# Column tiles for the query-key-value product, attended values a step later, style on ScalarE and merged exponent rounds

## What is computed

```python
def layer0(x, c, positions):                       # conditioned attention block
    sh1, sc1, g1, sh2, sc2, g2 = split(c @ ada_w.T + ada_b, 6)
    h = rmsnorm(x) * (1 + sc1) + sh1
    q, k, v = split(h @ qkv_w.T)                   # then q, k: rmsnorm by head, rotated by positions
    o = softmax(q @ k.T / sqrt(8)) @ v
    x = x + g1 * (o @ proj_w.T + proj_b)
    h2 = rmsnorm(x) * (1 + sc2) + sh2
    return x + g2 * (silu(h2 @ w1.T) * (h2 @ w3.T) @ w2.T)

def layer1(x, emb, gate):                          # linear attention
    q, k, v = layer_norm(x) @ (Wq, Wk, Wv) + (bq, bk, bv)
    y = softmax_d(q) @ (softmax_n(k).T @ v)
    h = layer_norm(y) * (1 + scale) + shift        # scale, shift = silu(emb) @ emb_W + emb_b
    return x + gate * (silu(h) @ out_W + out_b)
```

## Time and profile before

| what | before |
|---|---|
| median of three runs | 207.35 us |
| the profiled execution | 207.43 us, its span 205.4 us |
| TensorE (PE) busy | 180.9 us, 88% of the span |
| VectorE (DVE) busy | 166.1 us, 81% |
| GpSimd (POOL) busy | 141.3 us, 69% |
| ScalarE (ACT) busy | 129.4 us, 63% |
| granted TensorE clock | full in all 40 slices |
| chain that ended last, by engine | PE 40%, DVE 17%, issue 8%, POOL 5%, ACT 4% |

### The profile page before, as it was taken

How to read it: one execution, slowest core, us unless ns; L and a number is a source line. 1 busy time by engine, 2 the same in 40 slices (tenths; PEclk the granted TensorE clock), 3 DMA queues, 4 the chain that set the end, 5 groups by cost and what they waited for, 6 DMA issues and landing times.

```text
span 205.4 us, 6100 instructions
## 1 busy us (share of the span) xinstructions
PE 180.9 (88%) x2039; PEld 142.3 (69%) x2039; DVE 166.1 (81%) x498; ACT 129.4 (63%) x377; POOL 141.3 (69%) x333
## 2 busy tenths in 40 slices
PE   2598887997999999799999998899998899999963
PEld 2345565786687777677676777799997677888642
DVE  6699898896989999997776534668889799999882
ACT  1367798776867777576546763454442468999741
POOL 8889798998989797958810682434542847668651
PEclk9999999999999999999999999999999999999999
DMA  5955006800000000000000000000000000010111
GB/s 93 289 137 207 0 10 254 359 6 0 3 3 2 5 5 0 3 0 5 3 3 0 5 0 3 0 0 5 2 0 2 0 3 0 0 30 28 51 51 51
DMA packets 10428, 8.30 MB, mean 40 GB/s; under 512 B 3106, under 2 KB 9887, under 8 KB 9887
## 3 DMA queue, kind: packets, MB, share of 16 engines
q1 hardware_dynamic: 7006, 7.25, 10.3%
q10 hardware_dynamic: 3392, 0.68, 1.7%
HBM read 6.86 MB, written 1.07 MB: 39 GB/s over the span
## 4 chain that ended last, share of the span: by engine, by line
PE 40%; DVE 17%; issue 8%; POOL 5%; ACT 4%; POOLq 0%; ACTq 0%; DVEq 0%
PE bank L1895 5%; DVE qkpad L1604 5%; PE bank L875 5%; PE bank L1886 5%; PE bank L863 5%; PE bank L864 4%; PE bank L1975 4%; ACT probs L1302 2%; PE bank L908 2%; POOL rstd L515 2%; PE bank L1907 1%; PE bank L1920 1%; PE bank L992 1%; PE bank L1949 1%; PE bank L972 1%
## 5 line engine op out<-in xcount | busy, mean ns | idle before, releaser
L1604 DVE TENSOR_REDUCE qkpad<-bank 128x4 f32<-128x512 f32 x64 | 41.0, 684 | 10.1 <-PE bank L1886 9.2
L1302 ACT ACTIVATE probs<-bank 128x512 f32<-128x512 f32 x64 | 34.7, 594 | 22.6 <-PE bank L1895 22.5
L1895 PE MATMUL bank<-qTm,kBD 32*128 32x128 f32 x512 | 37.1, 283 | 0.1
L1886 PE MATMUL bank<-kBD,qTs 32*128 32x256 f32 x224 | 32.0, 399 | 4.4 <-DVE qkpad L1604 3.4
L1895 PEld LDWEIGHTS bank<-qTm,kBD 32*128 32x128 f32 x512 | 31.0, 186 | 0.9 <-issue 0.6
L1886 PEld LDWEIGHTS bank<-kBD,qTs 32*128 32x128 f32 x224 | 19.7, 184 | 10.3 <-DVE qkpad L1604 6.3
L575 ACT ACTIVATE th<-bank 128x256 f32<-128x256 f32 x24 | 9.2, 384 | 19.4 <-PE bank L864 16.0
L1975 PE MATMUL bank<-probs,vpad 128*32 128x128 f32 x512 | 18.6, 277 | 2.0 <-ACT probs L1302 2.0
L1975 PEld LDWEIGHTS bank<-probs,vpad 128*32 128x32 f32 x512 | 12.6, 109 | 8.4 <-ACT probs L1302 7.3
L1130 POOL TENSOR_TENSOR partner<-qk,rope 128x96 f32<-128x96 f32 x32 | 14.4, 471 | 2.0 <-ACT qk L1344 2.0
L1949 PE MATMUL bank<-qkvT,hT 128*128 128x384 f32 x32 | 15.3, 571 | 0.5 <-ACT hT L1319 0.5
(11 more groups left out here) (253 smaller groups left out, 521.4 us busy)
## 6 DMA issues: line engine op xcount, KB each, us to landing
gate<-in_cond_dram SPq DMA_DIRECT2D x1, 1024.0 KB, 4.7
x<-gate_rows SPq DMA_DIRECT2D x1, 1024.0 KB, 4.3
y<-gate_rows SPq DMA_DIRECT2D x1, 1024.0 KB, 6.4
res<-gate_rows SPq DMA_DIRECT2D x1, 1024.0 KB, 9.8
out_dram<-res SPq DMA_DIRECT2D x7, 128.0 KB, 1.8
xin<-in_x_dram ACTq DMA_DIRECT2D x2, 256.0 KB, 5.4
xin<-in_x_dram SPq DMA_DIRECT2D x1, 512.0 KB, 5.7
ada_n<-in_L_cond_ada_w_dram SPq DMA_DIRECT2D x1, 256.0 KB, 6.2
```

What stands on the lines that cost most here:

```text
L1302: q.activation(probs[2 * r + i][:, :, :, :].rearrange("p f a t -> p (f a t)"), bank[E_BANK[i]][:, :], ACT.Exp, scale=SCALE).then_inc(s_p, 1)
L1604: q.tensor_reduce(out_, score_bank(b, r, i)[:, :].rearrange("p (f a t) -> p f a t", f=2, a=2), X_AXIS, ALU.max, negate=True).then_inc(s_ma ...
L1886: last = q.matmul(bank[S_BANK[i]][:, f * 2 * T:(f + 1) * 2 * T], qTs[b % 2][rows, f, :], kBD[b % NKB][rows, f, :, :].rearrange("p a t -> p ...
L1895: last = q.matmul(bank[E_BANK[i]][:, (2 * f + k) * T:(2 * f + k + 1) * T], kBD[t % NKB][rows, f, k, :], qTm[t % 2][rows, f, :], start=True ...
```

## The change

The change has these parts:

- `queries_keys_values`: from sequence 6 on, the product is made in four tiles of 32 stationary columns each, with all 384 moving columns for each tile.
- `attended`, `projection`, `gated_projection`, `after_attention` and `spread_of` work on sequences one step older (t-2 and t-3), the attention loop has one step more (`LAST_A = B + 3`), and `oT` has two buffers. TensorE's `attended` stands behind round 0 and not ahead of the weighted values; ScalarE's stands between the two exponents of round 0.
- `queries_and_keys` and `input_turned` come directly behind that, ahead of `projection`, `token_major` and `queries_and_max`.
- The masked queries `qTs` of sequences from 3 on are made by ScalarE.
- In steps 14 and 15, where there are no scores left, one call `exponents` computes all inputs, with 4 row groups side by side; its second half goes to banks 0 and 1. The feed-forward chunks therefore use banks 4, 0, 1 and not 0, 1, 4, and chunks 1 and 2 wait for all exponents.
- `style`: one operation stays on VectorE, in step 0; the broadcast and the scaled weights are made on ScalarE at the end of step 10. `prepare_biases` moves to t = 11, 12 and 13.

```diff
-LAST_A, LAST_POOL = B + 2, B + 1
+LAST_A, LAST_POOL = B + 3, B + 1
...
-        GU_BANK, F_BANK, X_BANK = (0, 1, 4), (2, 3), 7
+        GU_BANK, F_BANK, X_BANK = (4, 0, 1), (2, 3), 7
...
+        def exp_bank(b, r, i):
+            return bank[(S_BANK if r == 1 and b + 2 >= B else E_BANK)[i]]
...
+                    if c > 0 and at(u, 0):
+                        e.wait_ge(s_p, NC * B)
...
+            def queries(b):
...
+                a.wait_ge(s_kb, b - MASKED_BY_ACT + 1)
+                q.activation(qTs[b % 2][:, :, :].rearrange("p f t -> p (f t)"), bank[T_BANK][:, 0:2 * T], ACT.Identity,
+                             scale=rowmask[:, 0:1]).then_inc(s_kq, 1)
...
             for t in range(LAST_A):
                 exp(t, 0, 1)
+                attended(t - 2)
                 exp(t, 0, 0)
...
+                modulated_input(t + 6)
                 queries_and_max(t + 1)
-                modulated_input(t + 6)
+                queries(t + 3)
                 exp(t, 1, 0)
                 exp(t, 1, 1)
-                if t < B:
-                    attended(t - 1)
...
-                spread_of(t - 2)
+                spread_of(t - 3)
                 if t == B - 6:
                     a.wait_ge(ld_rest, N_REST)
                     q.activation(outw[:, :], outw_n[:, :], ACT.Copy, scale=0.5).then_inc(pv_a, 1)
-            blocks_scalar(a, 2)
+                    q.activation(nbb[:, :], ident[:, :], ACT.Identity, bias=par[:, R_NB:R_NB + 1], scale=0.0).then_inc(pv_a, 1)
+                    q.activation(lin[:, :, :].rearrange("p c f -> p (c f)"), lin_n[:, :, :].rearrange("p c f -> p (c f)"), ACT.Identity,
+                                 scale=par[:, R_NG:R_NG + 1]).then_inc(pv_a, 1)
+            blocks_scalar(a, LAST_A - B)
...
                 rowmax(t + 2, 0, 1)
+                keys_apart(t + 3)
                 reciprocals(t - 1)
-                gated_projection(t - 2)
                 attended(t - 1)
-                keys_apart(t + 3)
-                queries(t + 3)
+                gated_projection(t - 3)
...
-                after_attention(t - 2)
+                after_attention(t - 3)
...
-                if t == B - 8:
                     style()
...
+            def exponents(t):
+                e.wait_ge(s_qTm, t + 1)
+                e.wait_ge(s_max, NC * B)
+                e.wait_ge(s_p, NC * t)
+                for f in range(2):
+                    for k in range(2):
+                        for r in range(2):
+                            for i in range(2):
...
+                    for c in range(4):
+                        last = q.matmul(front_bank(b)[32 * c:32 * c + 32, 128:512], hT[b % 2][:, 32 * c:32 * c + 32], qkvT[:, :],
+                                        start=True, stop=True)
...
             for t in range(LAST_A):
-                round_(t, 0)
-                projection(t - 2)
+                if t < B - 2:
+                    round_(t, 0)
+                elif t < B:
+                    exponents(t)
+                attended(t - 2)
+                queries_and_keys(t + 3)
+                input_turned(t + 6)
+                projection(t - 3)
                 token_major(t - 1)
...
-                queries_and_keys(t + 3)
-                input_turned(t + 6)
-                if B - 6 <= t < B - 3:
-                    prepare_biases(t - (B - 6))
+                if B - 5 <= t < B - 2:
+                    prepare_biases(t - (B - 5))
...
-                round_(t, 1)
+                if t < B - 2:
+                    round_(t, 1)
                 queries_keys_values(t + 6)
-                if t < B:
-                    attended(t - 1)
                 weighted_values(t, 0)
+                weighted_values(t, 1)
                 if t == B - 1:
                     b_rest(t - B, t % 2)
-                weighted_values(t, 1)
                 if t >= B:
                     b_input(t - B, t % 2)
                     b_rest(t - B, t % 2)
-                    attended(t - 1)
-            blocks_tensor(e, 2)
+            blocks_tensor(e, LAST_A - B)
```

More of the change, by code:

```diff
@@ L1361, in attended @@
                 a.wait_ge(s_oTp, b + 1)
-                wait(a, s_proj, b)
-                q.activation(oT[:, :], bank[P_BANK][:, 256:384], ACT.Copy).then_inc(s_oT, 1)
+                wait(a, s_proj, b - 1)
+                q.activation(oT[b % 2][:, :], bank[P_BANK][:, 256:384], ACT.Copy).then_inc(s_oT, 1)
             def summed(b):
@@ L1836, in prepare_biases @@
                 if part == 0:
[L1837 removed]
+                    e.wait_ge(pv_a, A_STYLE)
+                    e.wait_ge(pv_v, V_CSILU)
                     e.wait_ge(s_v, B)
@@ L1898, in round_ @@
                                     last.then_inc((s_e0, s_e1)[i], 1)
+            def exponents(t):
[6 more added lines that the diff above has]
+                            for i in range(2):
+                                row = 32 * (2 * r + i)
+                                rows = slice(row, row + 32)
+                                last = q.matmul(exp_bank(t, r, i)[:, (2 * f + k) * T:(2 * f + k + 1) * T], kBD[t % NKB][rows, f, k, :],
+                                                qTm[t % 2][rows, f, :], start=True, stop=True)
+                                if f == 1 and k == 1:
+                                    last.then_inc((s_e0, s_e1)[i], 1)
             def projection(b):
@@ L1904, in projection @@
                 e.wait_ge(s_oT, b + 1)
-                e.wait_ge(s_oT4, min(b + 2, B))
+                e.wait_ge(s_oT4, min(b + 3, B))
                 wait(e, s_x1g, b)
-                q.matmul(bank[O_BANK][:, 0:D], oT[:, :], projT[:, :], start=True, stop=True).then_inc(s_proj, 1)
+                q.matmul(bank[O_BANK][:, 0:D], oT[b % 2][:, :], projT[:, :], start=True, stop=True).then_inc(s_proj, 1)
             def token_major(b):
@@ L1948, in queries_keys_values @@
                 e.wait_ge(s_hT, b + 1)
-                q.matmul(front_bank(b)[:, 128:512], hT[b % 2][:, :], qkvT[:, :], start=True, stop=True).then_inc(s_qkv, 1)
+                if b < FRONT_B:
+                    q.matmul(front_bank(b)[:, 128:512], hT[b % 2][:, :], qkvT[:, :], start=True, stop=True).then_inc(s_qkv, 1)
+                else:
+                    for c in range(4):
+                        last = q.matmul(front_bank(b)[32 * c:32 * c + 32, 128:512], hT[b % 2][:, 32 * c:32 * c + 32], qkvT[:, :],
+                                        start=True, stop=True)
+                    last.then_inc(s_qkv, 1)
             def queries_and_max(b):
@@ L1966, in weighted_values @@
                     wait(e, s_on, b)
-                    wait(e, s_x1g, b - 1)
+                    wait(e, s_x1g, b - 2)
                     if b == 0:
@@ L1984, in attended @@
                 wait(e, s_qTm, min(b + 3, B))
+                wait(e, s_oT, b)
                 q.transpose(bank[P_BANK][:, 256:384], o[:, :, :].rearrange("p h d -> p (h d)"), ident[:, :]).then_inc(s_oTp, 1)
```

45 lines of the change are left out of this document (22 added, 23 removed).

## The result

The changed kernel takes 209.11 us (median of 12 runs, 208.92 to 209.94) against 207.37 us before: ratio 1.008, 95% interval 1.0062 to 1.0098. The forecast was 209.2. The profiled execution takes 209.30 us with a span of 207.57 (before 207.43 and 205.42).

A forecast was written before the change was run, and what follows sets the result against it. TensorE, busy 88%, was taken to wait for others, with ScalarE's exponents a 2.99 us floor under the half from round 1. Terms -1.06 + 1.38 + 0.64 - 0.43 + 1.29 = +1.82 on 207.43 gave 209.2 us, range 206.3 to 211.4.

The forecast's parts named there:

- the floor of 2.99: From round 1 to the next round 0, ScalarE's exponents allow no less than 2.99 us; 3.07 falls only to that.
- The rival that TensorE's saving counts: Front steps gain 0.3 us each, merged rounds 1.1 each, if exponents do not hold the values: 204.2 us; chance 0.12.
- that of strict order: Rival: column tiles run strictly one after another, the product takes 1.6 us, ten steps lose 7 us: 216; chance 0.04.
- First half longer by the evacuation: Round 0 to round 1: ScalarE's evacuation between the two exponents delays round 1, 2.66 us in place of 2.55, +0.11.
- Wait for GpSimd in step 3: Queries' and keys' transposes wait for GpSimd with more work queued behind them: +0.63 us, bounds 0 and 1.0.
- VectorE's relief: Masked queries moved to ScalarE shorten steps where VectorE makes seeds: -0.16, -0.09 and -0.26 us up to step 10.
- Style: Step 9: taking four operations off VectorE ahead of the row maxima removes TensorE's wait, -1.22 us.
- Steps 10 to 13: Bias products a step later, behind the queries' transposes, with two preparation pieces in step 13: 20.98 to 22.36 us, +1.38.
- Merged exponents: Steps 14 and 15: one TensorE round less each, but later work waits for four exponents: 13.77 against 13.13 us, +0.64.
- Steps 16 to 18 and the late square: TensorE's wait for its transposed output goes, -0.43 us; sequence 15's late squares delay GpSimd's normed input, fourth feed-forward step, +1.29.
- The rival that the square costs nothing: ScalarE reaches the squares before its last tanh, or GpSimd runs them in time; the 1.29 goes: 207.9 us; chance 0.20.
- the masked queries make ScalarE the bound: Rival: masked queries end after the exponents are due, each of 14 steps loses about 0.2 us more: 212.0; chance 0.16.

The follow-up runs named there:

- the one product: Changed kernel with the query-key-value product of sequences 6 to 15 as one product of 128 stationary columns again: median 210.32 us.
- the shorter exponents: Changed kernel with ScalarE's second exponent of round 1 covering 256 of 512 columns in steps 2 to 13 (output wrong): 206.94 us in one run.
- the preparation in the wait: Changed kernel with preparation products between the halves of the weighted values in steps 10 to 13, style on ScalarE in pieces: 206.75 us, ratio 0.9975.
- its edit: Changed kernel with GpSimd's normed input (normed1) ahead of its statistics (rms1) in the feed-forward loop: 207.95 us, ratio 1.0026.
- two swaps of two lines: Each on the changed kernel: GpSimd's normed input ahead of its statistics, 207.95 us; ScalarE's copy of the sums ahead of the tanh in step 15, 208.51 us.
- the small parts of a change alone: Kernel before with the style part alone: 206.13 us; with preparation products between the halves of the weighted values as well: 205.43 us.
- the mended whole: Changed kernel with preparation between the value halves, normed input ahead of statistics, sums' copy ahead of tanh: 204.27 us; split rounds instead of merged exponents and that copy: 204.64 us.

## Why the prediction was right

The total was nearer than its terms, and that is luck in part: up to round 1 of step 10 the sum was 0.35 us too high and in steps 10 to 13 it was 0.52 too low. 1.82 us was forecast; the medians differ by 1.74, the two traces by 2.15.

**TensorE's saving goes into a wait.** Held: the floor of 2.99 that I read from the earlier trace rows measured 2.96 to 2.99, and tiles or none made no difference. The Trainium skill, TensorEngine Tiling (Array Packing), "Key Properties", says that a change of tiling mode drains TensorE; that the values start 0.18 us sooner behind the tiles (0.67 against 0.85) agrees, but none of it came back as time. The rival that TensorE's saving counts falls with the one product and the shorter exponents; that of strict order falls by the 0.67 us from product to values.

**First half longer by the evacuation.** +0.11 forecast, +0.17 measured; it ate the 0.10 of the second half.

**Wait for GpSimd in step 3.** +0.63 forecast. The transposes start at 49.85 us (before 49.75), and round 1 comes 1.35 behind them (before 0.70), as worked out; from the start of the loop to this round 1 it is 0.52 longer, and the first half of the step alone 0.38 (3.83, 4.21). GpSimd does set it: in four traces of the kernels above the granted clock is 0.66 to 0.69 from 20 to 25 us and the loop starts 0.8 to 0.95 us later, and still this round 1 starts within 0.12 us of the changed kernel's.

**VectorE's relief.** The size was right by accident and the cause wrong: -0.16, -0.09 and -0.26 forecast, -0.32, -0.05 and -0.21 measured, with another -0.37 in step 4, which I had left out. Giving the queries back to VectorE took none of it away; what shortened step 6 stands in the last section.

**Style.** -1.22 forecast, -1.14 measured from round 1 of step 8 to that of step 9, and -1.24 in step 9 (6.86, 5.62) by itself.

**Steps 10 to 13.** +1.38 forecast, +1.90 measured. The mechanism held, as the preparation in the wait showed; the term was undersized in steps 11, 12 and 13 (6.43, 6.00 and 7.49 us for 6.26, 5.90 and 7.21). In step 13 the queries' transposes end 2.64 us after round 0 (109.14), not 2.37 as I had them, and that is the whole difference there.

**Merged exponents.** 13.77 forecast, 13.80 measured, and the copy behind the tanh was the cause of the whole loss: with the copy ahead it is 12.96, against 13.13 before.

**Steps 16 to 18 and the late square.** -0.43 and +1.29 forecast, -0.57 and +1.33 measured; the queue order as cause was shown by its edit. The rival that the square costs nothing fell. That the masked queries make ScalarE the bound was not seen: without them on it no step from 5 to 9 was shorter by more than 0.04 us.

**The range.** The widest bounds give 209.2 - 0.63 - 0.39 - 0.4 = 207.8 as the low end and not 208.0; nothing else rests on that.

## What to carry to other kernels

When one engine's work is cut, find what ends the same stretch a few hundredths of a us later; here it was another engine's exponents, and the gain turned into a wait that could then be filled with work that had to be done anyway. Behind a wait in the middle of a queue nothing is hidden, so it is the place in the order, not the step, that decides what small work costs. When a producer moves a step later, look at what stands behind its consumer on every in-order queue: two swaps of two lines gave back about 2 us. And try the small parts of a change alone on the old kernel: here they brought most of what the mended whole brought.

## What the hardware showed

VectorE's residual add of two SBUF operands (same instruction, 128x128) beside GpSimd, in the kernel before in steps 5 and 13:

```profile
64.61 0.73 POOL L1141 TENSOR_TENSOR rot<-qk,rope 128x256 f32<-128x256 f32 x1
64.66 0.83 DVE L1661 TENSOR_TENSOR x<-x1g,xin 128x128 f32<-128x128 f32 x1
...
112.65 0.28 DVE L1661 TENSOR_TENSOR x<-x1g,xin 128x128 f32<-128x128 f32 x1
```

In the changed kernel, step 5:

```profile
64.73 0.73 POOL L1148 TENSOR_TENSOR rot<-qk,rope 128x256 f32<-128x256 f32 x1
64.94 0.67 DVE L1675 TENSOR_TENSOR x<-x1g,xin 128x128 f32<-128x128 f32 x1
```

And in the kernel with the masked queries on VectorE, step 5:

```profile
64.39 0.73 POOL L1148 TENSOR_TENSOR rot<-qk,rope 128x256 f32<-128x256 f32 x1
...
64.91 0.36 DVE L1675 TENSOR_TENSOR x<-x1g,xin 128x128 f32<-128x128 f32 x1
```

With no GpSimd operation beside it the add takes 0.28 us. Started 0.05, 0.21 and 0.52 us after GpSimd's rotation it takes 0.83, 0.67 and 0.36: in all three it ends 0.15 us after the rotation. The Trainium skill, SBUF — State Buffer, "SBUF: two separate sides", says that a VectorE operation with two SBUF inputs and a GpSimd operation that reads SBUF exclude each other: the one that starts first holds the shared ports for its whole instruction. These rows agree.

This settles what shortened step 6. From the end of the add to round 1 of step 6 it is 2.69 us before (65.49 to 68.18) and in the changed kernel (65.61 to 68.30). But the add ends 0.27 us after round 0 of step 6 before (65.22), and 0.04 after it in the changed kernel (65.57), about the 0.22 us by which that half became shorter (2.96, 2.74). It also shows why VectorE's relief brought nothing there: in the changed kernel VectorE, free of the masked queries, starts the add 5.06 us after round 0 of step 5 and ends it at 5.73; with the masked queries it starts later, at 5.25, and still ends earlier, at 5.61, because the rotation ends earlier (5.46 against 5.58). Why GpSimd's rotation moved within the step, no run shows.

The clock: in the profiled execution of the one-product kernel, stretches 115 to 120 and 120 to 125 us; and the first of these in the changed kernel (the first figure behind POOL's is the granted clock).

```profile
115.00:120.00 5.00, 3.17 (x53) 2.01 (x45) 1.63 (x5) 3.31 (x8) 4.54 (x8) 0.91 0.01 3
120.00:125.00 5.00, 4.62 (x59) 3.80 (x59) 1.47 (x6) 3.06 (x10) 4.50 (x11) 0.75 0.00 0
```

```profile
115.00:120.00 5.00, 3.17 (x65) 2.19 (x60) 1.63 (x5) 3.63 (x10) 4.54 (x8) 1.00 0.00 0
```

Cut finer, the granted clock of the one-product kernel is 1.00 up to 119 us, 0.50 (1.2 of 2.4 GHz) from 119.5 to 122.5 and 1.00 from there on, so 0.91 and 0.75 above are means over both levels. With it, from round 1 of step 13 to the projection of step 16 it is 18.34 us in place of 16.79. From 115 to 119 us TensorE was equally busy in both executions (2.17 of 4 us); what sets the fall off stays open.
